# Attention on one core: the transposes of the exponential tiles are replaced by a second, transposed score matmul

## The reference, cut to what matters

```python
x = layernorm(x + L0(x, adj, ...))        # 8 steps h = h + dt * f(adj @ h, h @ w_eff, h, x0)
qkv = x @ W                               # q, k, v: 4 heads of 32
mask = where(adj == 0, -inf, 0)           # one 512 x 512 mask for every sample and head
scores = einsum('bhid,bhjd->bhij', q, k) / sqrt(32) + mask
attn = softmax(scores, axis=-1)
out = einsum('bhij,bhjd->bhid', attn, v)
x = layernorm(x + out)
```

## Time and profile before

| what | value |
|---|---|
| median of 3 runs | 736.59 us (735.1 to 737.56) |
| profiled execution, its own time | 734.45 us |
| span in the profile | 732.4 us |
| PE matmuls | 687.3 us busy (94%) |
| PE weight loads | 558.1 us busy (76%) |
| DVE | 417.4 us busy (57%) |
| ACT | 380.7 us busy (52%) |
| mean granted clock of PE | 0.981 |

### The profile page before, as it was taken

How to read it: one execution, slowest core, us unless ns; L and a number is a source line. 1 busy time by engine, 2 the same in 40 slices (tenths; PEclk the granted TensorE clock), 3 DMA queues, 4 the chain that set the end, 5 groups by cost and what they waited for, 6 DMA issues and landing times.

```text
span 732.4 us, 14091 instructions
## 1 busy us (share of the span) xinstructions
PE 687.3 (94%) x4753; PEld 558.1 (76%) x4753; DVE 417.4 (57%) x1229; ACT 380.7 (52%) x855; POOL 71.1 (10%) x85
## 2 busy tenths in 40 slices
PE   5999999999999999999999999999999999978674
PEld 3778988987888788878797788878887889654441
DVE  5440114555576475657575667557564757686863
ACT  3131124665556565556565555656456655665660
POOL 5010100201002000200020100200020000000000
PEclk9999999999999999999999999999999999997997
DMA  3000003030302221130304030312112120312210
GB/s 104 1 1 29 1 30 84 15 98 9 92 12 71 59 58 42 43 86 25 75 0 124 5 96 4 80 49 63 37 47 55 34 69 23 80 40 62 76 27 29
DMA packets 37058, 35.39 MB, mean 48 GB/s; under 512 B 7456, under 2 KB 24224, under 8 KB 37024
## 3 DMA queue, kind: packets, MB, share of 16 engines
q1 hardware_dynamic: 37024, 34.96, 18.4%
HBM read 5.57 MB, written 4.19 MB: 13 GB/s over the span
## 4 chain that ended last, share of the span: by engine, by line
PE 75%; DVE 7%; issue 6%; SPq 5%; DMA 4%; ACT 2%; DVEq 0%; POOLq 0%; POOL 0%; ACTq 0%
PE psL L614 12%; PE psE L714 12%; PE psO L725 8%; PE psS L654 7%; SPq L345 5%; PE psL L625 4%; PE psL L627 4%; PE psL L626 4%; PE psL L642 3%; PE psL L644 3%; PE psL L643 3%; DMA Ks<-kl 3%; PE psM L691 3%; DVE Sm L855 2%; DVE y L843 2%
## 5 line engine op out<-in xcount | busy, mean ns | idle before, releaser
L466 ACT ACTIVATE E<-Sm,negmax 128x512 f32<-128x512 f32 x256 | 182.8, 716 | 137.3 <-DVE negmax L855 137.3
L855 DVE CUSTOM_DVE_ANT_0 Sm<-psS,mask 128x512 f32<-128x512 f32 x256 | 166.3, 684 | 14.9 <-PE psS L654 9.9
L886 DVE COPY ET<-psE 128x512 f32<-128x512 f32 x116 | 79.8, 688 | 146.9 <-PE psE L714 146.8
L614 PE MATMUL psL<-R,zT 128*128 128x128 f32 x1152 | 142.1, 275 | 0.0
L714 PEld LDWEIGHTS psE<-ident,E 128*128 128x128 f32 x928 | 105.5, 143 | 44.3 <-issue 39.6
L614 PEld LDWEIGHTS psL<-R,zT 128*128 128x128 f32 x1152 | 137.0, 192 | 2.0 <-issue 0.2
L714 PE MATMUL psE<-ident,E 128*128 128x128 f32 x928 | 124.7, 278 | 2.5 <-DVE ET L886 1.5
L654 PE MATMUL psS<-Ks,Qs 96*128 96x512 f32 x256 | 96.4, 451 | 19.2 <-DVE negmax L855 9.2
L514 ACT ACTIVATE ET<-psE 128x512 f32<-128x512 f32 x116 | 68.9, 594 | 61.6 <-PE psE L714 61.4
L400 POOL TENSOR_TENSOR rstd<-var,minus_half 128x4 f32<-128x4 f32 x32 | 32.3, 1009 | 571.4 <-DVE var L838 571.4
L642 PE MATMUL psL<-Yh,PTh 128*128 128x256 f32 x256 | 72.7, 284 | 0.0
(11 more groups left out here) (127 smaller groups left out, 793.1 us busy)
## 6 DMA issues: line engine op xcount, KB each, us to landing
Qs<-qh SPq DMA_DIRECT2D x128, 64.0 KB, 2.0
Ks<-kh SPq DMA_DIRECT2D x128, 64.0 KB, 2.0
xin<-in_x_dram SPq DMA_DIRECT2D x8, 512.0 KB, 3.8
Qs<-ql SPq DMA_DIRECT2D x64, 64.0 KB, 2.0
Ks<-kl SPq DMA_DIRECT2D x64, 64.0 KB, 2.0
out_dram<-y SPq DMA_DIRECT2D x16, 256.0 KB, 2.3
...
```

The lines of the kernel that those rows point to most:

```text
L466: nc.scalar.activation(E[:, h % 2, i, :], Sm[:, i % 2, :], ACT.Exp, scale=-1.0, bias=negmax[:, h * NT + i:h * NT + i + 1], accum_out=sums[ ...
L614: last = mm(bank_ap[:, (t * GB + b) * D:(t * GB + b + 1) * D], zT[:, i, b, nodes], R[:, block * PW + i, :], start=False, stop=alone and t ...
L855: V_.tensor_tensor_reduce(out=Sm[:, i % 2, :], in0=psS[i % 2][:, :], in1=mask[:, i, :], scale=-SCALE, scalar=3e38, op0=ALU.add, op1=ALU.mi ...
L886: V_.tensor_copy(ET[:, n, i, :], e_bank(horner, i)[:, :]).then_inc(t_ev[1], 1)
```

## The change: what it does

The exponentials are no longer transposed. Instead a second matmul computes the scores in transposed form: `ST` (h, t) takes 128 keys of `Ks` as weights and streams all 512 queries of `Qs`. The maximum of each query has to be subtracted before the exponential, and in this form it lies along the free axis. So it comes in through the contraction: `Ks` gets two more rows of ones (partitions 96 and 97) and `Qs` two more rows that hold the negated maximum, divided by the scale, as a high and a low part. `ST` contracts over 98 rows. DVE adds the transposed mask `maskT` (ST's bank psT to `ET`), and ACT takes the exponential of `ET` in place. The first exponential stays, written over `Sm`, because its row sums are needed.

`MT` (h) makes the two rows: PE transposes the four columns of `negmax` (128 x 4) into 4 x 128, and that goes to the second score bank, `m_bank = psS[1]`. ACT writes `Mh`, DVE writes `Ml`, and SP moves each by a DMA of 4 x 128 numbers into row 96 or 97 of `Qs`. Since the bank is shared, the next head's second score matmul, `S` (h, 1), waits for `mt_lo`, which DVE raises when `Ml` is done.

The stacking is now an entry of the list, `STK` (h). It waits until the last `ST` of the old sample has read `Qs` and `Ks`, and for `kl`; its first six DMAs all stand behind `kl`. At the start there are 16 transposes of the adjacency matrix for `maskT`, and four more DVE instructions. `E` is gone, the startup tiles that lay in it now lie in `ET`.

```diff
-    ("TR", 0, 0), ("TR", 0, 1), ("S", 1, 0), ("S", 1, 1), ("LN1A", 0, 0),
+    ("S", 1, 0), ("MT", 0, 0), ("S", 1, 1), ("LN1A", 0, 0),
...
-    ("TR", 1, 0), ("TR", 1, 1), ("S", 2, 0), ("S", 2, 1), ("CB", 0, 0),
+    ("ST", 0, 0), ("ST", 0, 1), ("S", 2, 0), ("MT", 1, 0), ("S", 2, 1), ("CB", 0, 0),
...
+    ("HORNER", 6, 0), ("ST", 2, 0), ("ST", 2, 1), ("MT", 3, 0), ("S0", 0, 0), ("ST", 2, 2), ("ST", 2, 3),
+    ("HORNER", 7, 0), ("V", 3, 0), ("STK", 2, 0),
+    ("S0", 0, 1), ("S0", 0, 2), ("S0", 0, 3), ("ST", 3, 0), ("ST", 3, 1),
+    ("HORNER", 8, 0), ("ST", 3, 2), ("ST", 3, 3), ("STK", 3, 0),
...
+        m_bank = psS[1]
...
SP:
+                for kind, n, i in events(j, horner, prep, attend, end):
...
+                    elif kind == "MT":
+                        sp.wait_ge(mt_lo, a * H + n + 1)
+                        for row, part in enumerate((Mh, Ml)):
+                            sp.dma_start(f(Qs[KS + row:KS + row + 1, n, :]), f(part[:, n % 2, :])).then_inc(mt_in[n], 16)
+                    elif kind == "STK":
                         if attend:
-                            sp.wait_ge(s_mm, s_unit(it - ATT, h, NT))
-                        if h == 0:
-                            sp.wait_ge(m_ev, MPB * (it - PREP) + 2)
-                        stack(Qs, (qh, ql, qh), h)
-                        if h == 0:
-                            sp.wait_ge(m_ev, MPB * (it - PREP) + 3)
-                        stack(Ks, (kh, kh, kl), h)
+                            sp.wait_ge(st_mm, s_unit(a, n, NT))
+                        if n == 0:
+                            sp.wait_ge(m_ev, MPB * p + 3)
+                        stack(Qs, (qh, ql, qh), n)
+                        stack(Ks, (kh, kh, kl), n)
+                    elif kind == "LN2B":
+                        store()
...
ACT:
-                nc.scalar.activation(E[:, h % 2, i, :], Sm[:, i % 2, :], ACT.Exp, scale=-1.0,
+                nc.scalar.activation(Sm[:, i % 2, :], Sm[:, i % 2, :], ACT.Exp, scale=-1.0,
...
+                    elif kind == "MT":
+                        act.wait_ge(mt_mm, a * H + n + 1)
...
+                        nc.scalar.activation(Mh[:, n % 2, :], m_bank[0:NT, 0:P], ACT.Copy,
+                                             scale=1 / SCALE).then_inc(mt_hi, 1)
+                    elif kind == "ST":
+                        act.wait_ge(st_add, s_unit(a, n, i) + 1)
+                        nc.scalar.activation(ET[:, n, i, :], ET[:, n, i, :], ACT.Exp, scale=SCALE).then_inc(st_exp, 1)
...
PE:
+                if i == 1 and (not isinstance(rows_taken, int) or rows_taken > 0):
+                    pe.wait_ge(mt_lo, rows_taken)
...
+            def transposed_scores(a, h, t):
+                s = s_unit(a, h, t)
+                if t == 0:
+                    pe.wait_ge(mt_in[h], 32 * (a + 1))
+                if t >= 2 or not isinstance(s, int) or s >= 2:
+                    pe.wait_ge(st_add, s - 1)
+                mm(psT[t % 2][:, :], Ks[0:KT, h, t * P:(t + 1) * P], Qs[0:KT, h, :],
+                   start=True, stop=True).then_inc(st_mm, 1)
...
+                    elif kind == "MT":
+                        pe.wait_ge(s_max, s_unit(a, 1 if n == 0 and not horner else n, NT))
...
+                        nc.tensor.transpose(m_bank[0:NT, 0:P], negmax[:, n * NT:(n + 1) * NT],
+                                            ident[:, :]).then_inc(mt_mm, 1)
...
                     elif kind == "PV":
                         if n == 0:
-                            for part_ev in t_ev:
-                                pe.wait_ge(part_ev, H * NT // 2 * (e + 1))
+                            pe.wait_ge(st_exp, s_unit(e, H, 0))
...
DVE:
+                    elif kind == "MT":
+                        dve.wait_ge(mt_hi, a * H + n + 1)
+                        V_.scalar_tensor_tensor(out=Ml[:, n % 2, :], in0=m_bank[0:NT, 0:P], scalar=1 / SCALE,
+                                                in1=f(Mh[:, n % 2, :]), op0=ALU.mult,
+                                                op1=ALU.subtract).then_inc(mt_lo, 1)
+                    elif kind == "ST":
...
+                        V_.tensor_tensor(ET[:, n, i, :], psT[i % 2][:, :], maskT[:, i, :], ALU.add).then_inc(st_add, 1)
```

More of the change, by code:

```diff
@@ L32 @@
 KS = 3 * HD
+KT = KS + 2
 IPG = GB
@@ L228, in gnn_kernel @@
         R_BANKS = [psL[0], psL[1], psO]
-        P_BANKS = psS + psE
+        P_BANKS = psS + psT
+        m_bank = psS[1]
         in_w = sem("in_w")
@@ L275, in gnn_kernel @@
         s_exp = sem("s_exp")
-        t_mm = sem("t_mm")
-        t_ev = [sem("t_ev0"), sem("t_ev1")]
+        mt_mm = sem("mt_mm")
+        mt_hi = sem("mt_hi")
+        mt_lo = sem("mt_lo")
+        mt_in = [sem(f"mt_in{h}") for h in range(H)]
+        a_mm = sem("a_mm")
+        ones_in = sem("ones_in")
+        st_mm = sem("st_mm")
+        st_add = sem("st_add")
+        st_exp = sem("st_exp")
         o_mm = sem("o_mm")
@@ L330, in iteration @@
                 it = g * IPG + j
-                if horner and j == 0 and not is_last(g):
-                    sp.wait_ge(l0_mm, UPG * g + GB)
-                    sp.wait_ge(x_split, (g + 1) * GB)
-                    sp.dma_start(xin[:, :, :, :], x_v[:, bass.ds((g + 1) * GB, GB)]).then_inc(xin_in, 16)
+                a, p = it - ATT, it - PREP
                 def store():
@@ L508, in iteration @@
                     elif kind == "S":
-                        exponential(a, 1 - j, n, i, False)
+                        exponential(a, 1 - j, n, i)
                     elif kind == "S0":
-                        exponential(p, j, n, i, not attend)
-                    elif kind == "TR" and i % 2 == 0:
-                        act.wait_ge(t_mm, s_unit(a, n, i) + 1)
-                        nc.scalar.activation(ET[:, n, i, :], e_bank(horner, i)[:, :], ACT.Copy).then_inc(t_ev[0], 1)
+                        exponential(p, j, n, i)
+                    elif kind == "MT":
+                        act.wait_ge(mt_mm, a * H + n + 1)
+                        if n < 2:
+                            for m_in in mt_in[2:]:
+                                act.wait_ge(m_in, 32 * a)
+                        else:
+                            act.wait_ge(mt_in[n - 2], 32 * (a + 1))
+                        nc.scalar.activation(Mh[:, n % 2, :], m_bank[0:NT, 0:P], ACT.Copy,
[3 more added lines that the diff above has]
+                        nc.scalar.activation(ET[:, n, i, :], ET[:, n, i, :], ACT.Exp, scale=SCALE).then_inc(st_exp, 1)
                     elif kind == "OT":
@@ L597, in _ @@
             last.then_inc(bias_mm, 1)
+            pe.wait_ge(pt_lo, PW * NT)
+            for m in range(NT):
+                for t in range(NT):
+                    last = nc.tensor.transpose(P_BANKS[m][:, t * P:(t + 1) * P],
+                                               adj_sb[:, t, m * P:(m + 1) * P], ident[:, :])
+                last.then_inc(a_mm, 1)
             pe.wait_ge(in_qkv, 16)
@@ L633, in join @@
                 step, m = n // UPS, n % UPS
-                if isinstance(g, int) and g == 0:
-                    pe.wait_ge(pt_lo, PW * NT)
                 for k in range(NT):
@@ L651, in scores @@
                     pe.wait_ge(stacked[h], 6 * 16 * (a + 1))
+                    if isinstance(a, int) and a == 0 and h == 0:
+                        pe.wait_ge(c_vec, 5 + NT)
+                        pe.wait_ge(ones_in, 1)
+                if i == 1 and (not isinstance(rows_taken, int) or rows_taken > 0):
+                    pe.wait_ge(mt_lo, rows_taken)
                 if not fresh or i >= 2:
@@ L817, in _ @@
             V_.tensor_scalar(mask[:, :, :], adj_sb, 0.0, NEG, ALU.is_equal, ALU.mult).then_inc(c_vec, 1)
-            dve.wait_ge(c_vec, 5)
+            for m in range(NT):
+                dve.wait_ge(a_mm, m + 1)
+                V_.tensor_scalar(maskT[:, m, :], P_BANKS[m][:, :], 0.0, NEG, ALU.is_equal, ALU.mult).then_inc(c_vec, 1)
+            dve.wait_ge(c_vec, 5 + NT)
             dve.wait_ge(rt_ev, 3)
```

75 lines of the change are left out of this document (30 added, 45 removed), and 29 rows, old and new, of tables (EVENTS, LATE_EVENTS).

## The result

The changed kernel takes 1041.62 us (median of 4 runs, 1036.25 to 1043.87), the kernel before 736.21: ratio 1.414, 95% interval 1.410 to 1.419. It is slower, as forecast, but by 305 us and not by 239, and 1.6 us beyond the end of the range.

The account below looks back on a forecast made before the run. PE was taken to bound the middle iterations, 39.55 us each. 734.45 + 165 (middle waits less saved PE work) + 45 (clock) + 26 (late) + 2 (start) = 972.5, so 975 us; range 885 to 1040 us.

Parts of the forecast that it names:

- PE's own work: Middle iteration: 64 transposes go, 16 `ST` and four `MT` come; PE's work falls by 2.2 us.
- three `mt_lo` waits: Slots 0, 2 and 4: PE's second score matmul waits for `Ml`, 2.6, 3.2 and 3.2 us; 9.0 us an iteration.
- the four others: Middle iteration: PE waits before `S0` (0, 0), `S0` (0, 3), `ST` (3, 0) and next `PV`; 6.3 us, 0.4 already there.
- clock: Middle iteration: waits drop PE to 1.2 GHz in three stretches of 1.2 us cost each; 3.5 us, 45 us in 13.
- The rival that they would be hidden: Middle iterations: only the `mt_lo` waits are real, the four others are taken up; 887 us, chance 0.12.
- the fourth case: Middle iterations: clock stays low for much of each, 9 us instead of 3.5; 1046 us, chance 0.10.
- the third case: Middle iterations: only the `mt_lo` waits count, the four others vanish; 887 us, chance 0.12.
- Late iterations: Three late iterations: DVE's added work, `mt_lo` chain and waits for SP add 9, 9 and 8 us; 26 us (10 to 40).
- Start: At the start, 16 transposes cost PE 2 us.
- Rival "not slower": At `mt_lo`: `Mh` and `Ml` come early, PE does not wait, only its work counts; 710 us, chance 0.03.

Follow-up runs that it names:

- E12: E9 with nine unread matmuls per j = 0 iteration, 3 ahead of `S0` (0, 0) and 6 ahead of `S0` (0, 3): 783.59 us.
- E8: Changed kernel with DVE's `ql` pass of slot 4 moved behind the slot's last score tile: 1016.39 us.
- E2: Changed kernel with 40 unread 128x512 matmuls behind `MT` in each full middle iteration: 974.27 us.
- E11: E7 with seven unread 128x512 matmuls put into each of its three added waits: 816.29 us.
- E7: Kernel before, with the second score matmul of slots 0, 2 and 4 made to wait for the first tile's exponential: 838.15 us.
- E10: E9 with unread 128x512 matmuls added in each late iteration: 789.84 us.
- E9: Changed kernel reordered (`MT` first, `ST` a slot earlier, `Qs` DMAs earlier, late order), with polynomial pieces between the tiles of slots 6 to 8: 788.21 us.
- E6: Changed kernel with only the late iterations reordered, moving `MT`, `ST` and the rows of `MT` (3): 1033.9 us.
- E1: Changed kernel with the middle iterations' four `MT` entries moved to the front of their slots: 850.48 us.

## Why the prediction was right in its sign and short in its size

Each step for one middle iteration, in us:

| step | forecast | measured |
|---|---|---|
| PE's own work | -2.2 | -1.8 (E12) |
| three `mt_lo` waits | 9.0 | 9.8 (18.1 / 2, and 3 x 0.25) |
| the four others, less 0.4 that was there | 5.9 | 6.3 (11.4 / 2, and 4 x 0.25, less 0.4) |
| clock | 3.5 | 5.9 (what is left of 20.2) |
| sum | 16.2 | 20.2 |

- **PE's work.** Right: the second matmuls are cheaper than the transposes. The 13 iterations would have gained about 23 us if nothing waited.
- **`mt_lo`.** Right in mechanism, place and chain, and nearly in size. By slot the rows and 0.25 us for each give 2.5, 3.0 and 4.2 to 4.4 us, where 2.6, 3.2 and 3.2 were forecast. Slot 4's excess is the `ql` pass, which the forecast left out; E8 moved it and the waits fell by 1.05 us in an iteration. (The forecast has 0.74 us from DVE's maximum to the exponential in slots 2 and 4, where the earlier trace rows have 0.82; the rows above have 0.73.)
- **The four other waits.** Right in kind and in sum. In the rows, with the forecast in brackets: `S0` (0, 0) 2.3 (2.0), `S0` (0, 3) 1.3 with j = 0 and 1.0 with j = 1 (1.2), `PV` 1.7 in the mean (1.9). `ST` (3, 0) waits 0.9 us with j = 1 and not at all with j = 0 (1.2 in each). The rival that they would be hidden is refuted by their rows.
- **The clock: the step that failed.** "I take three such stretches in an iteration at 1.2 us each" was too small. The mean of 0.86 over 119.56 us means 33 us at 1.2 GHz in two iterations (119.56 x 0.14 x 2), so 17 us in one, where I had three stretches of about 3 us. Two things were missing. The clock stays low for several microseconds of full PE behind a wait, 5.5 us behind slot 4's. And it falls in more places: eight times in the two iterations, for 3.4 to 7 us each, behind the waits of slots 2 and 4, in slot 7, and once each behind `PV` and slot 0. Where PE is full, each such microsecond costs about half of itself. The term was bounded at 9 us and I took less than half of that; the measured 5.9 lies about halfway between the forecast and the fourth case (1046 us). It is rather low than high: PE is busy 45.0 us in an iteration, and 37.3 for the same work at full clock in E12, which puts the term at up to 7.7, as that difference also holds the modelled ends. Over 13 iterations the miss is 31 of the 67 us. That the fourth case's time came within 5 us is luck in part: its clock term is larger than the measured one, and the other terms below made up for it. The range, meant to run from the third case to the fourth, stopped 6 us short of it, and the time fell into that gap.
- That the term exists, three experiments show: E2 and E11 add work on PE and save 67 and 22 us, and E7 has the low clock with nothing of the change. The Trainium skill (TensorE: Matmul & The Clock Gate, section "A second HAM failure mode: psum-queue depth-cycling") says that frequent short idling between groups of matmuls makes the clock swing between two levels. The traces agree: 1.00 and 0.50 alternate in the two iterations shown of the changed kernel, with a mean of 0.86.
- **Late iterations.** 35.7 us instead of 26. DVE's busy time there rose by 5 us in an iteration, of the 6.4 forecast (28.15 in the row below, 23.10 before), and the other 7 to 9 us are chains in which DVE waits for PE's score matmuls, for `ST` and for ACT's `Mh`:

```profile
948.49:992.73 44.24, 27.70 (x89) 12.82 (x89) 28.15 (x82) 24.89 (x58) 2.58 (x3) 0.65 0.17 43
```

```profile
DVE Sm L882 <- PE psS L677: 15.7, 6, 4.1
DVE ET L920 <- PE psT L686: 7.1, 4, 3.3
DVE Ml L913 <- ACT Mh L524: 6.3, 5, 1.6
```

  The waits are those of two late iterations, 904.31 to 992.73. How much of them is PE's clock of 0.65 stays open: the only run that raised a late clock, E10, did it on E9's order, where DVE hardly waited for PE. Two new orders (E6, E9) took 7 and 11 us away. In E9 25 us are left; DVE's added work is 15 us in the three late iterations, and what the other 10 are is not settled.
- **Start.** 4.9 us instead of 2. Of it 2.0 are the first score matmul's wait for the stacking, 3.73 us where it was 1.70; the rest was not examined.
- **Rival "not slower".** It needed `Ml` early. E1, E9 and E12 made it early, and even in the best of them, E12, two middle iterations took 80.9 us and not the 74.7 of PE's own work: they were still 1.8 us longer than before, and the late part 26.

The pieces add up: the clock 31 us; `mt_lo` 0.8, the others 0.4 and PE's work 0.4 in an iteration, 21 in 13; late 10; start 3. That is 65 of the 67 us.
